# A second graph layer gives one of its 64 relu units per tile from VectorE to ScalarE

## The reference

```python
# first layer
fa = einsum('btc,oc->bto', feat, W1a); fb = einsum('btc,oc->bto', feat, W1b)
h = relu(fa[:, :, None, :] + fb[:, None, :, :])
att = einsum('bijo,o->bij', h, W2)
att = softmax(att + where(adj > 0, 0.0, NEG_INF)); out = einsum('bij,bjc->bic', att, feat)
# second layer
vu = edge_attr @ U2; iv = edge_attr @ W2
lr = leaky_relu(vu[:, :, None, :] + iv[:, None, :, :], 0.2)
scores = where(edge_adj > 0, einsum('bijc,c->bij', lr, yita), -1e12)
agg = leaky_relu(einsum('bij,bjc->bic', softmax(scores), edge_attr), 0.2)
emb = leaky_relu((agg + (1 + beta) * edge_attr) @ linW.T + linb, 0.2)
# both: x = layernorm(x + ...)
```

## Time and profile before

| | |
|---|---|
| median of 3 runs | 5830.69 us (5829.75 to 5830.9) |
| the profiled execution's own time | 5828.89 us |
| its span, first to last instruction | 5826.4 us |
| busy over the span | PE 5530.6, DVE 5404.7, ACT 5129.8, POOL 906.6 us |
| mean granted TensorE clock | 0.967 |

### The profile page before, as it was taken

How to read it: one execution, slowest core, us unless ns; L and a number is a source line. 1 busy time by engine, 2 the same in 40 slices (tenths; PEclk the granted TensorE clock), 3 DMA queues, 4 the chain that set the end, 5 groups by cost and what they waited for, 6 DMA issues and landing times. The chain is left out here.

```text
span 5826.4 us, 138045 instructions
## 1 busy us (share of the span) xinstructions
PE 5530.6 (95%) x58164; PEld 2225.6 (38%) x58164; DVE 5404.7 (93%) x8136; ACT 5129.8 (88%) x6073; POOL 906.6 (16%) x889
## 2 busy tenths in 40 slices
PE   8999999999999999999999999997778889888888
PEld 2333333333333333333333333333444445444444
DVE  8999999999999999999999999996768899889988
ACT  8999999999999999999999999985858888888887
POOL 0000000000000111111211111111302222222223
PEclk9999999999999999999999999997879999999999
DMA  1000000000000000000000000002511111011100
GB/s 42 19 19 20 16 19 19 19 16 19 19 19 16 19 19 16 19 19 16 19 19 16 19 16 19 19 12 82 150 38 28 32 32 32 25 32 32 35 22 18
DMA packets 144490, 156.45 MB, mean 27 GB/s; under 512 B 51782, under 2 KB 119110, under 8 KB 143878
## 3 DMA queue, kind: packets, MB, share of 16 engines
q1 hardware_dynamic: 143238, 147.55, 9.1%
q10 hardware_dynamic: 640, 0.07, 0.0%
HBM read 137.10 MB, written 2.10 MB: 24 GB/s over the span
## 5 line engine op out<-in xcount | busy, mean ns | idle before, releaser
L323 DVE TENSOR_SCALAR a_hidden<-a_B,a_A 128x1024 f32<-128x1024 f32 x4992 | 3592.2, 793 | 85.1 <-PE apsS L214 66.0
L249 ACT ACTIVATE a_hidden<-a_B,a_A 128x1024 f32<-128x1024 f32 x3200 | 3424.5, 1139 | 200.7 <-PE apsS L214 197.0
L214 PE MATMUL apsS<-a_hidden,a_w_sel 128*32 128x512 f32 x32768 | 3560.3, 593 | 11.4 <-DVE a_hidden L323 11.2
L214 PEld LDWEIGHTS apsS<-a_hidden,a_w_sel 128*32 128x32 f32 x32768 | 1044.4, 110 | 2424.5 <-issue 2036.1
L652 PE MATMUL m3S<-xT,Q 64*128 64x512 f32 x2048 | 615.0, 674 | 90.9 <-ACT x_even L696 61.9
L696 ACT ACTIVATE x_even<-m3S,bias 128x512 f32<-128x512 f32 x684 | 433.2, 687 | 209.2 <-PE m3S L652 184.8
L668 PE MATMUL m3O<-ZT,Xr 32*64 32x256 f32 x16384 | 573.5, 411 | 4.3 <-DVE ZT L745 4.3
L668 PEld LDWEIGHTS m3O<-ZT,Xr 32*64 32x64 f32 x16384 | 356.4, 142 | 326.5 <-issue 240.0
L745 DVE STREAM_TRANSPOSE ZT<-x_even 128x1024 f32<-128x1024 f32 x342 | 422.4, 1238 | 57.9 <-ACT x_even L705 53.2
L736 DVE CUSTOM_DVE_ANT_0 x_even<-x_even,mask 128x1024 f32<-128x1024 f32 x342 | 428.8, 1289 | 38.5 <-ACT x_even L696 38.4
L705 ACT ACTIVATE x_even<-x_even,low 128x1024 f32<-128x1024 f32 x342 | 393.7, 1151 | 0.0
(11 more groups left out here) (157 smaller groups left out, 3180.4 us busy)
## 6 DMA issues: line engine op xcount, KB each, us to landing
a_adj_in<-adj SPq DMA_DIRECT2D x128, 512.0 KB, 3.6
adj_in<-adj SPq DMA_DIRECT2D x128, 512.0 KB, 4.0
Xr<-x_odd SPq DMA_DIRECT2D x128, 64.0 KB, 3.0
out<-yn SPq DMA_DIRECT2D x64, 32.0 KB, 1.5
x_even<-x SPq DMA_DIRECT2D x1, 256.0 KB, 2.9
wqT<-L_wqT SPq DMA_DIRECT2D x1, 130.0 KB, 2.6
wkT<-L_wkT SPq DMA_DIRECT2D x1, 130.0 KB, 2.7
wvT<-L_wvT SPq DMA_DIRECT2D x1, 130.0 KB, 2.8
```

Of the source, the lines that this page charges most:

```text
L214: last = pe.matmul(psS[k % 2][32 * q:32 * q + 32, h * HALF:(h + 1) * HALF], w["sel"][layer][:, 30 - 2 * p:62 - 2 * p], hidden[:, (k * GROU ...
L249: act.activation(hidden[:, (k * GROUPS + p) % SLOTS, q, :], B2[:, g % 2, :], ACT.Relu, bias=A2[:, g % 2, pair:pair + 1]).then_inc(hid_act, 1)
L323: dve.tensor_scalar(hidden[:, (k * GROUPS + p) % SLOTS, q, :], B2[:, g % 2, :], A2[:, g % 2, pair:pair + 1], 0.0, ALU.add, ALU.max).then_i ...
```

## The change

In the second layer ACT also makes q = 2 of group p = 4: 26 units for ACT and 38 for DVE in each of its 64 tiles. The first layer stays at 25 and 39. What PE waits for is now counted with the layer in mind.

```diff
-def act_share(g):
-
-    return (2, 3) if g % 2 or g == 8 else (3,)
...
+def act_share(layer, g):
+
+    return (2, 3) if g % 2 or g == 8 or (layer and g == 4) else (3,)
...
+    def act_until(k, p):
+        layer = k // (nb * tiles)
+        whole = sum(nb * tiles * act_made(i, GROUPS - 1) for i in range(layer))
+        return whole + k % (nb * tiles) * act_made(layer, GROUPS - 1) + act_made(layer, p)
+
+    def dve_until(k, p):
+        return 4 * (k * GROUPS + p + 1) - act_until(k, p)
...
-                pe.wait_ge(hid_dve, k * DVE_PER_TILE + dve_made(p))
-                pe.wait_ge(hid_act, k * ACT_PER_TILE + act_made(p))
+                pe.wait_ge(hid_dve, dve_until(k, p))
+                pe.wait_ge(hid_act, act_until(k, p))
...
-                for q in act_share(p):
+                for q in act_share(g // nb, p):
...
-                    if q not in act_share(p):
+                    if q not in act_share(g // nb, p):
```

More of the change, by code:

```diff
@@ L23, with act_made @@
 SLOTS = 6
-def act_share(g):
-    return (2, 3) if g % 2 or g == 8 else (3,)
[L31 to L41, removed]
+def act_share(layer, g):
+    return (2, 3) if g % 2 or g == 8 or (layer and g == 4) else (3,)
+def act_made(layer, g):
+    return sum(len(act_share(layer, i)) for i in range(g + 1))
 def additive_layers(nc, adj, X, rest, w, buf, small, ident, nb, n):
```

## The result

The changed kernel takes 5812.64 us (median of 8 runs, 5805.61 to 5818.64) against 5830.08 us for the kernel before on the same chip (8 runs, 5824.94 to 5834.64). The ratio is 0.997, with a 95% interval of 0.996 to 0.9981: about 0.3% faster, where 5814.2 us was forecast. The profiled execution took 5811.58 us for a span of 5809.3.

What follows compares the result with a forecast made beforehand. DVE was taken to bound the second layer's full batch (251.30 us), PE close behind at 249.75. Stalls of 0.4 + 6.3 + 2.1 + 7.7 = 16.5 us off 5830.7 gave 5814.2 us, range 5811.5 to 5820.

Steps and rivals of the forecast that it cites:

- POOL's mask: Second layer: DVE loses 2.9 us a tile where POOL's two mask operations run, of about 4.1 if wholly blocked.
- What comes back: PE's stalls in the second layer, by turn starts: batch 9 0.4, batches 10 to 13 6.3, batch 14 2.1, last 7.7 us.
- The last term: Last batch of the second layer up to its last tile's turn: 190.35 us against a floor of 182.7, 7.7 us back.
- DVE's lead: Ring of six groups: some 4.4 us of lead left at the worst place; DVE falls back 3.7 us in the last batch.
- The price of 1.04 us: Cost of one ACT unit from start to start, 8.3 us a batch for the added units; ACT 238.9 of 249.75 busy.
- ACT bound: Rival: at 1.14 us a unit ACT needs 257.1 us a full second-layer batch, kernel 5875 us; 3 in 100.
- The cover of the exponentials: ACT's exponentials end 2.8 us before PE's turn in the first layer; the new unit uses at most 1.04, costed at nothing.
- All of DVE's time: Rival: PE's floor is soft and all 42.4 us of DVE's second-layer work come back, kernel 5788 us; 3 in 100.
- DVE late in part: Rival: lead used up, last batch above all; a quarter to two thirds of 16.5 us stay, 5818 to 5825; 12 in 100.
- Nothing moves: Rival: the stalls pass to another waiter, such as exponentials delayed by the unit at p = 4; 5829 to 5833 us; 5 in 100.

## Why the prediction was right

**What bounded the second layer.** DVE, with PE 1.55 us a batch behind: shown from both sides. In full batches less work on PE alone did nothing before the change and gave its full 3.5 us after it; less work on DVE by another way, POOL's mask, gave the same 249.75 us.

**What comes back.** Term by term against the turns: batch 9 0.4 (0.4), batches 10 to 13 6.3 (6.3), batch 14 2.1 (2.1), last batch 7.7 (6.9). The last term was mis-sized by 0.7 us: one stall is left, in the last of the six tiles (30.38 us in place of 29.65), 0.52 us of it in the row at 3935.41. It is not a fixed size: with the same division it came to 0.15 us in the run with 26 units in both layers. The median lies 1.6 us below the forecast although the turns gave 0.8 us less than it: that closeness is luck within the spread.

**DVE's lead.** The estimate put 4.4 us of room against the 3.7 us by which DVE falls back in the last six tiles, and so no stall. The start of masked_min, in a tile of the changed kernel where DVE waited for slots (turn at 3048.93) and in the last tile (turn at 3948.59), shows what was missed:

```profile
3040.79 1.22 DVE L332 CUSTOM_DVE_ANT_0 a_Z<-apsS,a_mask 128x1024 f32<-128x1024 f32 x1
```

```profile
3945.88 1.21 DVE L332 CUSTOM_DVE_ANT_0 a_Z<-apsS,a_mask 128x1024 f32<-128x1024 f32 x1
```

With the ring full DVE leads the turn by 8.1 us; when it holds PE up, by 2.7, as in the plain tile of the kernel before (3238.12 to 3240.76). So the room is 5.4 us, more than estimated. But at the turn that opens the last six tiles the lead is 5.8 us and not 8.1: the end of batch 14 has used 2.3 of it (the estimated 2 us of a batch's last tiles), and the last batch, with few jobs of PE, doesn't give it back. That leaves 3.1 us of room against 3.7. The step that was off is to have set the whole room against the last batch alone. A group of ring less, 1.7 us, cost 3.0 us (2.6 in the six tiles, 0.4 in batch 14); why more than 1.7 was not tried. The text allowed a microsecond or two there, and that is where it came.

**POOL's mask.** The second operation alone is recorded with 2.69 us and cost DVE 2.1 us; with both, 2.9 of some 4.1. The exclusive lock of the Trainium skill (SBUF — State Buffer, Who interferes with whom) agrees with the kind of loss. Part of what is missing is POOL's own waiting. The mask operation of the first layer at the start of the kernel, where DVE rests, in the kernel before:

```profile
15.43 1.04 POOL L123 TENSOR_SCALAR a_mask<-a_adj_in 128x1024 f32<-128x1024 int32 x1 [0.29 <-DMA a_adj_in<-adj]
```

It takes 1.04 us there and 1.42 beside DVE's units. If each operation of the second layer holds such a wait of 0.4 us, an estimate, some 3.3 us are left for DVE to lose against the 2.9 measured. What hides the rest was not tried.

**ACT.** The price of 1.04 us held (30.73 us for a plain tile with 28 units), so the rival of an ACT bound at 26 was out. By that rival's own terms the unit would bind from 1.10 us on, not from 1.12; nothing hangs on it. The rule of the Trainium skill (ScalarE: Activation LUTs, Rules for kernel authors) that relu belongs on VectorE would have argued against the change; the runs here show that with DVE full and ACT resting, the slower engine takes it for nothing up to 27 units, and not at 28. The cover of the exponentials came out at 2.3 us in the plain tile of the changed kernel:

```profile
3202.82 1.14 ACT L278 ACTIVATE a_Z<-a_Z,small 128x1024 f32<-128x1024 f32 x1
3203.86 0.19 ACT L278 ACTIVATION_READ_ACCUMULATOR a_Z<-a_Z,small 128x1 f32 x1
```

From 3204.05 to the turn at 3206.35; 2.8 less at most 1.04 was forecast.

**The rivals.** All of DVE's time: refuted by 27 units. DVE late in part: true for 0.7 us, far from its quarter. Nothing moves, ACT bound: refuted. What the prediction had too narrow is the spread of the runs: it gave 1.2 us from three, and eight runs of one kernel cover 9.7 us before and 13.0 after, which is nearly the size of the gain. The turn spacings tell what the times alone leave at 0.2 to 0.4%.

## What to carry to other kernels

Where several engines feed one, cost the change by the distance between the busiest engine and the next, batch by batch, from the starts of a repeating instruction and not from busy times: here the step from 24 to 25 units on ACT is worth 40 us, the one to 26 17 us, the one to 27 nothing. Find the floor of the next engine in a stretch where nothing is late, and compare tile by tile. A ring lets a late engine be paid back only within its length: an engine whose sum fits over a batch can still stall in the tiles where it is late (28 units: 1.4 us a batch over the sum), and a tail batch, where the other engines have less to do, can hold nearly half of the gain.

## What the runs showed of the hardware

Up to about 3950 us the clock is granted in full, and the turn spacing of a full batch is 249.75 us in every kernel here where PE sets the pace and has its full work; only the start of the whole series moves, by up to 1.8 us. The later layers do not repeat like that. From the turn in the last tile to the end of the span, the same work took 1867.9 us in the run with the unit at p = 6 and 1858.7 in the one with one mask operation:

```profile
3949.76:5817.70 1867.94, 1602.66 (x21852) 890.18 (x21852) 1538.93 (x2433) 1463.23 (x2364) 498.22 (x658) 0.89 0.17 44
```

```profile
3948.56:5807.30 1858.74, 1589.17 (x21854) 887.23 (x21852) 1534.62 (x2428) 1459.02 (x2362) 498.36 (x658) 0.90 0.17 44
```

The mean granted clock, 0.89 and 0.90 of full, differs the same way. So it does over the eight executions of the changed kernel: mean clocks of 0.966 go with 5816.3, 5816.3 and 5818.6 us, 0.967 with 5813.7, 0.968 with 5808.6 to 5811.6 and 0.969 with 5805.6. Whether it is the whole cause was not tried; it isn't an effect of the change, since the stretches of before and after (1862.1 and 1860.7 us) lie between the two.
